# Layer norms of a twelve-block network: the reciprocal root of the variance as a power on GpSimd

## The chip, the cores and the metric

The kernel runs on one core of one Trainium2 chip. The metric is the device time of one launch in microseconds. The profile is one execution of the same program, taken by the hardware profiler.

## What is computed

The input x has shape (32, 32, 128), that is 1024 tokens of 128 features. Twelve blocks in four layers (cross attention, self attention, feed-forward; the feed-forward blocks of layers 0 to 2 mix gated experts) are each added to x, and each takes x normalised over its features:

```python
def _layernorm(x, axis=-1, eps=1e-05):
    m = jnp.mean(x, axis=axis, keepdims=True)
    v = jnp.var(x, axis=axis, keepdims=True)
    return (x - m) / jnp.sqrt(v + eps)
...
x = x + _L3_attn_ref(_layernorm(x, axis=-1), ...)
```

There are six inner norms too. The self attention of layer 3 adds a second norm of its (already normalised) input, with scale and shift, to its output; the self attention of layer 0 normalises its heads' output; the cross attention of layer 2 has two inner norms; the self attention of layer 2 has two that divide by the plain standard deviation (eps 0). With the 12 outer ones that makes 18 norms; "norm 1" to "norm 18" number them in program order. Norm 3 is the inner one of the layer 0 attention, norm 4 that of the layer 0 feed-forward block, norm 15 that of the layer 3 cross attention, and norms 16 and 17 are the two of the layer 3 self attention.

## The kernel before

All activations stay on chip. X, XN, Y, Z and ACC hold the 1024 tokens as 8 tiles of 128 tokens by 128 features (`NT = 8`), tokens on partitions. MV holds mean and variance of each tile (128x8x2), SD two rows of 8 values a partition: the variance plus eps, then the standard deviation and its reciprocal. The order on each engine is written out by hand in five blocks, one an engine, and engines wait for each other only through counted semaphores. So an instruction that waits holds up all that follows it on its engine.

A norm runs like this. VectorE makes the statistics (`bn_stats`, L1327) of 8 tiles and aggregates them (`bn_aggr`, L1336). `layernorm` adds eps to the 8 variances (L1340, raises `var_ready`), waits for `std_ready`, takes the reciprocal (L1343) and writes 8 normalised tiles (L1346). ScalarE's part is `norm_std` (its operations are recorded at L940): it loads the table of the root ahead of time by an operation on one column (`prepare(ACT.Sqrt)`), waits for `var_ready`, takes the root, and prepares the function that the stage wants next. TensorE turns each normalised tile as it comes (`turn`, L431), and ScalarE copies the turned halves to XNT or ZT (L959).

Two norms stand in a particular order. In the layer 0 feed-forward block (norm 4) ScalarE first scales four results of `weight_products(1)`; TensorE's `turn(XN)` waits for the same four (`y_w_taken`). In the layer 3 self attention `self_attention(..., True)` has two norms: ScalarE takes the first root, copies the turned halves, then copies q, k and v out of PSUM (L940, L1174, L1176), and only then takes the second root. VectorE, after the second norm's tiles and two affine operations on Z (L1323), spreads q over the heads in `heads()` (L1323 with a mask as second input, waits for the copy of q), and TensorE's scores (L743) wait for that.

GpSimd (the `@block.gpsimd` block) issues the loads of weights and rows at the start, then runs per stage: the staging of queries (L2022), bias additions to X (`bias`, L2011), expert biases (L2072, L2075), half of the divisions of a softmax (`divide`, L2062) and, in the cross attentions, `spread` (L2093 to L2121). Most of these wait for `norm_ready`, which the 8 tiles of an outer norm raise.

Of the kernel before, what the change touches and what calls it, by code (L numbers as in the profile page):

```python
# [16 lines left out]
ALU = mybir.AluOpType  # L17
ACT = mybir.ActivationFunctionType
# [5 lines left out]
NT = B * S // P  # L24
# [5 lines left out]
DK = 8  # L30
# [4 lines left out]
LN_EPS = 1e-5  # L35
# [84 lines left out]
def perceiver(nc, ctxT, ctxN, fside, mask, wpack, wrows, l1x_w, units, relb, x_in, out):  # L120
    ctx = ExitStack()
    with ctx:
# [6 lines left out]
        X = sb("X", [P, NT, P])  # L129
        XN = sb("XN", [P, NT, P])  # L130
# [32 lines left out]
        def ar(a, n):  # L163
            return AR[:, a:a + n]
# [8 lines left out]
            var_ready std_ready norm_ready stream_ready turned turned_taken  # L173
# [762 lines left out]
        def _(act):  # L936
            seen = Tally(act)

            def f(o, i, fn=ACT.Identity, **k):
                return act.activation(o, i, fn, **k)  # L940

            def prepare(fn):

                f(SM[:, 592:593], ident[:, 0:1], fn).then_inc(sig["act_ran"], 1)
                act.wait_ge(sig["act_ran"], seen.up("act_ran"))

            def norm_std(then=None):

                prepare(ACT.Sqrt)
                act.wait_ge(sig["var_ready"], seen.up("var_ready"))  # L950
                f(SD[:, 1, :], SD[:, 0, :], ACT.Sqrt).then_inc(sig["std_ready"], 1)
                act.wait_ge(sig["std_ready"], seen.up("std_ready"))
                if then:
                    prepare(then)

# [53 lines left out]
            norm_std(ACT.Exp)  # L1009
# [26 lines left out]
            norm_std(ACT.Exp)  # L1036
# [23 lines left out]
            norm_std()  # L1060
# [4 lines left out]
            norm_std(ACT.Sigmoid)  # L1065
# [7 lines left out]
            norm_std(ACT.Exp)  # L1073
# [94 lines left out]
            def self_attention(scale, second_norm=False):  # L1168
                norm_std(None if second_norm else ACT.Exp)
                turned(XNT[:, :])  # L1170
                act.wait_ge(sig["lin_ready"], seen.up("lin_ready"))
                f(c_q, PSF[:, 1024:2048], scale=scale).then_inc(sig["qkv_taken"], 1)
                act.wait_ge(sig["qkv_taken"], seen.up("qkv_taken"))
                act.copy(c_k, PSF[:, 2048:3072]).then_inc(sig["qkv_taken"], 1)  # L1174
                act.wait_ge(sig["qkv_taken"], seen.up("qkv_taken"))
                act.copy(c_vt, PSF[:, 3072:4096]).then_inc(sig["qkv_taken"], 1)  # L1176
                act.wait_ge(sig["qkv_taken"], seen.up("qkv_taken"))
                if second_norm:
                    norm_std(ACT.Exp)
                core()  # L1180
# [5 lines left out]
            norm_std(ACT.Exp)  # L1186
# [65 lines left out]
            norm_std(ACT.Exp)  # L1252
            turned(XNT[:, :])
            cross(None)
            norm_std(LAYERS_FF["l2x"][1])
            turned(ZT[:, :])
            ff("l2x")
            norm_std()


            norm_std(ACT.Exp)
# [22 lines left out]
            norm_std()  # L1284
# [4 lines left out]
            norm_std()  # L1289


            norm_std()
# [12 lines left out]
            norm_std(ACT.Exp)  # L1305
            turned(XNT[:, :])
            cross("l3x_bk")
            self_attention(float(DK) ** -0.5, True)
            norm_std(LAYERS_FF["l3f"][1])
# [9 lines left out]
        def _(dve):  # L1319
# [11 lines left out]
            def layernorm(src, dst, eps, signal=True, stats_done=False):  # L1331

                if not stats_done:
                    stats(src, range(NT))
                for t in range(NT):
                    dve.bn_aggr(MV[:, t, :], ST[:, t, :]).then_inc(sig["dve_ran"], 1)  # L1336
                    seen.up("dve_ran")
                    if t == NT - 1:
                        dve.wait_ge(sig["dve_ran"], seen.up("dve_ran", 0))
                dve.tensor_scalar(SD[:, 0, :], MV[:, :, 1], eps, None, ALU.add).then_inc(sig["var_ready"], 1)  # L1340
                dve.wait_ge(sig["var_ready"], seen.up("var_ready"))
                dve.wait_ge(sig["std_ready"], seen.up("std_ready"))
                dve.reciprocal(SD[:, 1, :], SD[:, 1, :]).then_inc(sig["dve_ran"], 1)  # L1343
# [156 lines left out]
            layernorm(X, XN, LN_EPS)  # L1500
# [42 lines left out]
            layernorm(X, XN, LN_EPS, stats_done=True)  # L1543
# [39 lines left out]
            layernorm(v3(lv), Z, 1e-5, signal=False)  # L1583
# [8 lines left out]
            layernorm(X, XN, LN_EPS, stats_done=True)  # L1592
# [15 lines left out]
            layernorm(X, XN, LN_EPS, stats_done=True)  # L1608
# [142 lines left out]
            layernorm(X, XN, LN_EPS, stats_done=True)  # L1751
# [6 lines left out]
            layernorm(X, XN, LN_EPS, stats_done=True)  # L1758
# [132 lines left out]
            layernorm(X, XN, LN_EPS, stats_done=True)  # L1891
# [6 lines left out]
            layernorm(Y, Z, 1e-5, signal=False, stats_done=True)  # L1898
# [5 lines left out]
            layernorm(ACC, Z, 1e-5, signal=False, stats_done=True)  # L1904
# [7 lines left out]
            layernorm(X, XN, LN_EPS)  # L1912
# [20 lines left out]
            layernorm(Y, Z, 0.0, stats_done=True)  # L1933
# [3 lines left out]
            layernorm(ACC, Y, 0.0, signal=False, stats_done=True)  # L1937
# [4 lines left out]
            layernorm(X, XN, LN_EPS)  # L1942
# [19 lines left out]
            layernorm(X, XN, LN_EPS)  # L1962
# [7 lines left out]
            layernorm(X, XN, LN_EPS, stats_done=True)  # L1970

            layernorm(XN, Z, 1e-5, signal=False)
# [10 lines left out]
            layernorm(X, XN, LN_EPS, stats_done=True)  # L1983
# [8 lines left out]
        def _(pool):  # L1992
            seen = Tally(pool)

            for g in ("l0", "l1", "l2", "l3"):
                a, cols = SPANS["group_" + g]
                if g == "l1":
                    pool.dma_start(RB[:, :, :], wrows.rearrange("a r n -> (a) r n").broadcast_to([P, len(ROWS), P])
                                   ).then_inc(sig["rows_landed"], 16)
                    pool.dma_start(MK[:, 0:2, :], mask[0:2 * P, :].rearrange("(c p) b -> p c b", c=2))\  # L2000
                        .then_inc(sig["mask_landed"], 16)
                    pool.dma_start(MK[:, 2, :], mask[2 * P:KEYS, :].broadcast_to([P, B]))\
                        .then_inc(sig["mask_landed"], 16)
                pool.dma_start(W[:, a:a + cols], wpack[:, a:a + cols]).then_inc(sig["w_" + g], 16)
            pool.wait_ge(sig["w_l0"], 16)
# [24 lines left out]
            seen.up("expert_weights")  # L2030

# [20 lines left out]
            seen.up("yu_taken", 2)  # L2052
            seen.up("norm_ready", NT)
# [26 lines left out]

            pool.wait_ge(sig["norm_ready"], seen.up("norm_ready", NT))
# [63 lines left out]

            pool.wait_ge(sig["norm_ready"], seen.up("norm_ready", NT))
# [6 lines left out]
            spread(False)  # L2153

            divide()
            pool.wait_ge(sig["c_out"], seen.up("c_out", 4))
            for u in range(11, H):
                pool.dma_start(*to_tokens(u)).then_inc(sig["pair_out_pool"], 16)
            seen.up("norm_ready", 2 * NT)


            pool.wait_ge(sig["norm_ready"], seen.up("norm_ready", NT))
# [3 lines left out]

            pool.wait_ge(sig["norm_ready"], seen.up("norm_ready", NT))
            bias("l3x_bo")
            spread(True)
            pool.wait_ge(sig["norm_ready"], seen.up("norm_ready", NT))  # L2170
            bias("l3a_bp")
            divide()
            pool.wait_ge(sig["norm_ready"], seen.up("norm_ready", NT))
# [168 lines left out]
```

## Time and profile before

| | |
|---|---|
| median of 3 runs | 1430.46 us (1424.09 to 1431.08) |
| the profiled execution's own time | 1426.8 us |
| its span in the trace | 1425.0 us |
| busy: TensorE, VectorE, ScalarE, GpSimd | 79%, 53%, 42%, 22% of the span |
| mean granted clock of TensorE | 0.859 of full speed |

The span runs from the first to the last instruction; 1.8 us of the execution's time lie around it. Busy shares are averages over stages with different limits: an engine with 22% can hold up the others wherever they wait for it.

### The profile page before, as it was taken

The numbers are of one execution on the slowest core, as the hardware profiler recorded it, in microseconds if no ns is written. First come the engines' busy times: TensorE is split into PE (matmuls) and PEld (weight loads), VectorE is DVE, ScalarE is ACT, GpSimd is POOL, SyncE is SP. The second block draws the span as 40 slices with busy tenths as digits, with TensorE's granted clock in tenths as the row PEclk, the third lists the DMA queues.
The fourth block names the chain that finished last, engine by engine and source line by source line (L and its number), as shares of the span: only waits on it lengthen the run. The fifth ranks groups of instructions, "written<-read, shape, count | busy, mean of one in ns | idle before, by whom it ended". The sixth has DMA issues, their size and how long they took to land. (4 is left out here: it accounts for less than half of the span.)

```text
span 1425.0 us, 26568 instructions
## 1 busy us (share of the span) xinstructions
PE 1130.6 (79%) x8781; PEld 839.4 (59%) x8781; DVE 750.7 (53%) x2071; ACT 592.0 (42%) x1226; POOL 311.4 (22%) x498
## 2 busy tenths in 40 slices
PE   5758998999996368999965233899999979998537
PEld 2325665878774346788843232577676758886434
DVE  2264444554554944566657494433333346665682
ACT  2133223433432133788842211434444348886122
POOL 1000001111120104555510010404032125554010
PEclk8577998999998568999977566899999989998557
DMA  8510120222220003455500201021111201111000
GB/s 270 142 60 1 35 63 18 57 60 52 56 60 1 2 1 97 120 144 138 148 0 1 45 2 37 28 62 45 45 56 45 71 8 31 30 30 31 1 1 15
DMA packets 70989, 75.04 MB, mean 53 GB/s; under 512 B 6272, under 2 KB 63696, under 8 KB 70536
## 3 DMA queue, kind: packets, MB, share of 16 engines
q1 hardware_dynamic: 67864, 66.18, 17.3%
q0 software_dynamic: 1152, 6.97, 1.4%
q10 hardware_dynamic: 1904, 0.98, 0.4%
q8 instruction: 42, 0.69, 0.2%
q14 instruction: 27, 0.22, 0.0%
HBM read 71.49 MB, written 0.52 MB: 51 GB/s over the span
## 5 line engine op out<-in xcount | busy, mean ns | idle before, releaser
L472 PEld LDWEIGHTS PS<-WB,AR 128*128 128x128 f32 x1568 | 189.4, 192 | 43.6 <-issue 40.7
L472 PE MATMUL PS<-WB,AR 128*128 128x128 f32 x1568 | 189.6, 275 | 0.0
L940 ACT ACTIVATE AR<-PS,WB 128x512 f32<-128x512 f32 x160 | 110.0, 687 | 156.0 <-PE PS L460 149.5
L817 PE MATMUL PS<-AR 128*128 128x257 f32 x512 | 149.3, 395 | 0.1
L1435 DVE SCALAR_TENSOR_TENSOR ACC<-PS,SM,ACC 128x128 f32<-128x128 f32 x256 | 72.2, 345 | 125.7 <-PE PS L472 124.4
L460 PE MATMUL PS<-ZT,WB 128*128 128x512 f32 x208 | 103.8, 624 | 3.5 <-ACT ZT L959 3.5
L817 PEld LDWEIGHTS PS<-AR 128*128 128x128 f32 x512 | 87.7, 191 | 20.0 <-issue 11.1
L1323 DVE TENSOR_TENSOR AR<-PS,AR 128x512 f32<-128x512 f32 (+2 forms) x69 | 48.4, 702 | 91.1 <-issue 39.4
L940 ACT ACTIVATE AR<-PS 128x512 f32<-128x512 f32 (+2 forms) x81 | 43.8, 541 | 121.7 <-PE PS L463 68.0
L460 PE MATMUL PS<-XNT,WB 128*128 128x512 f32 x168 | 89.3, 639 | 5.2 <-ACT AR L940 3.9
L940 ACT ACTIVATE AR<-PS,SM 128x257 f32<-128x257 f32 x136 | 64.8, 476 | 39.3 <-DVE SM L1507 28.8
L431 PE MATMUL PS<-W,XN 128*128 128x128 f32 x96 | 26.6, 450 | 61.9 <-DVE XN L1346 61.9
L940 ACT ACTIVATE AR<-AR 128x1024 f32<-128x1024 f32 (+1 forms) x39 | 46.3, 1188 | 70.0 <-DVE AR L1323 54.2
L754 PE MATMUL PS<-AR 32*32 32x128 f32 x768 | 30.5, 367 | 55.9 <-DVE AR L1725 55.9
L1847 DVE COPY AR<-PS 128x512 f32<-128x512 f32 x64 | 44.3, 692 | 52.6 <-PE PS L826 52.6
L940 ACT ACTIVATE AR<-AR,SM 128x257 f32<-128x257 f32 x128 | 65.3, 510 | 15.9 <-DVE SM L1832 10.5
L2093 POOL TENSOR_TENSOR AR<-AR,W 128x512 f32<-128x512 f32 x64 | 67.0, 1047 | 21.2 <-POOL OT L2121 15.0
L2042 POOL TENSOR_TENSOR AR<-AR,SM 128x516 f32<-128x516 f32 x32 | 33.7, 1054 | 159.1 <-ACT SM L940 93.9
L826 PE MATMUL PS<-W,AR 128*128 128x128 f32 x512 | 66.6, 273 | 2.3 <-ACT AR L940 2.2
L2011 POOL TENSOR_TENSOR X<-X,RB 128x1024 f32<-128x1024 f32 x6 | 14.1, 2345 | 242.8 <-DVE XN L1346 242.5
L2062 POOL TENSOR_TENSOR AR<-AR,SM 128x512 f32<-128x512 f32 x12 | 16.9, 1412 | 221.5 <-DVE SM L1703 221.0
L826 PEld LDWEIGHTS PS<-W,AR 128*128 128x128 f32 x512 | 59.5, 141 | 9.8 <-ACT AR L940 3.5
(225 smaller groups left out, 2207.2 us busy)
## 6 DMA issues: line engine op xcount, KB each, us to landing
WB<-in_units SPq DMA_DIRECT2D x49, 385.0 KB, 3.1
CTX<-in_fside SPq DMA_DIRECT2D x32, 514.0 KB, 4.1
CTX<-in_ctxT SPq DMA_DIRECT2D x96, 130.0 KB, 2.1
CTX<-in_ctxT SPq DMA_DIRECT2D x8, 520.0 KB, 4.5
CTX<-in_ctxN SPq DMA_DIRECT2D x16, 258.0 KB
CTX<-in_ctxN SPq DMA_DIRECT2D x32, 129.0 KB, 2.3
AR<-in_ctxN SPq DMA_DIRECT2D x32, 64.5 KB, 2.9
AR<-in_l1x_w POOLq DMA_DIRECT2D x1, 2048.0 KB, 8.2
```

Source lines behind the costliest of these rows:

```text
L431: m = pe.transpose(PS[:, t // 4, 128 * (t % 4):128 * (t % 4) + 128], src[:, t, :], ident)
L460: m = pe.matmul(bank(2 * c), WB[:, q, 128 * c:128 * c + 128], src[:, 512 * hh:512 * hh + 512], start=True, stop=True)
L472: m = pe.matmul(PS[:, 4 + hh, 128 * t:128 * t + 128], f_h[hh][:, c, 128 * t:128 * t + 128], WB[:, q, 2 * UNIT + 128 * c:2 * UNIT + 128 * c ...
L754: m = pe.matmul(PS[32 * g:32 * g + 32, 4 * half + b, P * tt:P * tt + P], c_vt[32 * b:32 * b + 32, at:at + 32], pt[32 * b:32 * b + 32, g, t ...
L817: m = pe.matmul(PS[:, 2 + g, 0:KEYS], x_qb[q][:, P * g:P * g + P], x_k[q], start=True, stop=True)
L826: m = pe.transpose(PS[:, 6 + c, P * g:P * g + P], x_p[q][:, g, P * c:P * c + P], ident)
L940: return act.activation(o, i, fn, **k)
L1323: return dve.tensor_tensor(o, a, b, op)
L1435: ins = dve.scalar_tensor_tensor(out=a, in0=y, scalar=f_w[:, 4 * hh + t, bass.ds(e, 1)], in1=a, op0=ALU.mult, op1=ALU.add)
L1847: dve.tensor_copy(x_pt[:, 1, :], PS[:, 7, :]).then_inc(sig["xpt_d"], 1)
L2042: pool.tensor_tensor(y_T[k % 2], y_last[k].unsqueeze(1).broadcast_to([P, HG, FQ]), y_pl[:, :, k].unsqueeze(2).broadcast_to([P, HG, FQ]), A ...
L2093: pool.tensor_tensor(x_qb[q].rearrange("p (h q) -> p h q", h=H), qv, m16, ALU.mult)\
```

## The change

Root and reciprocal leave ScalarE and VectorE. GpSimd gets a function `rstd`: when all 8 aggregates are there (each now raises `var_ready`), it adds eps to the variances and raises the sums to the power -0.5, with an exponent tile of eight values -0.5 in SM; VectorE waits for `rstd_ready`. `norm_std` is gone; where it prepared a next function, ScalarE now calls `prepare` alone, without waiting for the variance. In GpSimd's program a call of `rstd` stands for each of the 18 norms, ahead of the wait for that norm's tiles.

```diff
-            def norm_std(then=None):
-
-                prepare(ACT.Sqrt)
-                act.wait_ge(sig["var_ready"], seen.up("var_ready"))
-                f(SD[:, 1, :], SD[:, 0, :], ACT.Sqrt).then_inc(sig["std_ready"], 1)
-                act.wait_ge(sig["std_ready"], seen.up("std_ready"))
-                if then:
-                    prepare(then)
...
-            norm_std(ACT.Exp)
+            prepare(ACT.Exp)
             turned(XNT[:, :])
...
-                if second_norm:
-                    norm_std(ACT.Exp)
                 core()
...
                 for t in range(NT):
-                    dve.bn_aggr(MV[:, t, :], ST[:, t, :]).then_inc(sig["dve_ran"], 1)
-                    seen.up("dve_ran")
-                    if t == NT - 1:
-                        dve.wait_ge(sig["dve_ran"], seen.up("dve_ran", 0))
-                dve.tensor_scalar(SD[:, 0, :], MV[:, :, 1], eps, None, ALU.add).then_inc(sig["var_ready"], 1)
-                dve.wait_ge(sig["var_ready"], seen.up("var_ready"))
-                dve.wait_ge(sig["std_ready"], seen.up("std_ready"))
-                dve.reciprocal(SD[:, 1, :], SD[:, 1, :]).then_inc(sig["dve_ran"], 1)
-                dve.wait_ge(sig["dve_ran"], seen.up("dve_ran"))
+                    dve.bn_aggr(MV[:, t, :], ST[:, t, :]).then_inc(sig["var_ready"], 1)
+                dve.wait_ge(sig["rstd_ready"], seen.up("rstd_ready"))
...
+            def rstd(eps=LN_EPS):
+
+                pool.wait_ge(sig["var_ready"], seen.up("var_ready", NT))
+                pool.tensor_scalar(SD[:, 0, :], MV[:, :, 1], eps, None, ALU.add).then_inc(sig["pool_ran"], 1)
+                pool.wait_ge(sig["pool_ran"], seen.up("pool_ran"))
+                pool.tensor_tensor(SD[:, 1, :], SD[:, 0, :], SM[:, 504:512], ALU.pow).then_inc(sig["rstd_ready"], 1)
+                pool.wait_ge(sig["rstd_ready"], seen.up("rstd_ready"))
+            pool.memset(SM[:, 504:512], -0.5).then_inc(sig["pool_ran"], 1)
+            pool.wait_ge(sig["pool_ran"], seen.up("pool_ran"))
+            rstd()
...
             spread(True)
+            rstd()
             pool.wait_ge(sig["norm_ready"], seen.up("norm_ready", NT))
+            rstd()
             bias("l3a_bp")
```

## Rows read from the trace of the kernel before

**Rows 1.** The page, TensorE's busy time, its share of the span, its instructions.

```profile
PE 1130.6 (79%) x8781; PEld 839.4 (59%) x8781; DVE 750.7 (53%) x2071; ACT 592.0 (42%) x1226; POOL 311.4 (22%) x498
```

**Rows 2.** The tile SD: durations in ns (least/median/most), then its engines' idle time before.

```profile
L1340 DVE TENSOR_SCALAR SD<-MV x18: 171/172/172, 8.1 to 1390.0; 128x8 f32<-128x8 f32 x18
L940 ACT ACTIVATE SD<-SD x18: 208/208/209, 8.4 to 1390.3; 128x8 f32<-128x8 f32 x18
L1343 DVE RECIPROCAL SD<-SD x18: 202/203/204, 8.7 to 1390.6; 128x8 f32<-128x8 f32 x18
...
  DVE SD L1340: 92.7, 16
  ACT SD L940: 19.7, 18
```

**Rows 3.** Timeline of norms 16 and 17: start, duration (us), instruction, idle before.

```profile
1320.51 0.64 DVE L1336 BATCH_NORM_AGGREGATE MV<-ST 128x2 f32<-128x6 f32 x8
...
1322.00 2.14 DVE L1346 TENSOR_SCALAR XN<-X,MV,SD 128x128 f32<-128x128 f32 x8
...
1324.28 2.35 POOL L2011 TENSOR_TENSOR X<-X,RB 128x1024 f32<-128x1024 f32 x1 [10.21 <-DVE XN L1346]
...
1325.85 0.64 DVE L1336 BATCH_NORM_AGGREGATE MV<-ST 128x2 f32<-128x6 f32 x8
...
1333.78 1.02 ACT L940 ACTIVATE AR<-PS 128x1024 f32<-128x1024 f32 x1 [8.44 <-PE PS L765]
...
1335.88 1.01 ACT L1176 COPY AR<-PS 128x1024 f32<-128x1024 f32 x1
...
1337.47 0.20 DVE L1343 RECIPROCAL SD<-SD 128x8 f32<-128x8 f32 x1 [10.77 <-ACT SD L940]
...
1339.88 2.48 DVE L1323 TENSOR_TENSOR Z<-Z,RB 128x1024 f32<-128x1024 f32 x2
1342.40 4.62 DVE L1323 TENSOR_TENSOR AR<-AR,W 128x2048 f32<-128x2048 f32 x2
...
1344.84 0.44 PE L743 MATMUL PS<-AR 32*32 32x128 f32 x4 [11.15 <-DVE AR L1323]
```

**Rows 4.** Timeline of norm 4.

```profile
117.81 0.64 DVE L1336 BATCH_NORM_AGGREGATE MV<-ST 128x2 f32<-128x6 f32 x8
...
119.59 0.60 ACT L940 ACTIVATE AR<-PS 128x512 f32<-128x512 f32 x1 [0.22 <-PE PS L590]
...
120.68 1.28 ACT L940 ACT_TABLE_LOAD   x1
120.76 0.20 DVE L1343 RECIPROCAL SD<-SD 128x8 f32<-128x8 f32 x1 [2.11 <-ACT SD L940]
...
121.50 2.18 PE L431 MATMUL PS<-W,XN 128*128 128x128 f32 x8 [2.00 <-DVE XN L1346]
...
123.77 0.59 ACT L959 COPY XNT<-PS 128x512 f32<-128x512 f32 x1 [0.59 <-PE PS L431]
```

**Rows 5.** Timeline of norm 15, VectorE's reciprocal.

```profile
1150.90 0.20 DVE L1343 RECIPROCAL SD<-SD 128x8 f32<-128x8 f32 x1 [0.79 <-ACT SD L940]
```

**Rows 6.** Timeline of the end of the layer 3 cross attention.

```profile
1312.70 0.25 DVE L1860 SCALAR_TENSOR_TENSOR AR<-PS,SM,AR 128x32 f32<-128x32 f32 x1
1313.09 0.32 POOL L2110 TENSOR_TENSOR AR<-AR 128x64 f32<-128x64 f32 x1 [3.01 <-DVE AR L1860]
1313.49 0.25 POOL L2116 TENSOR_TENSOR AR<-AR 128x32 f32<-128x32 f32 x1
1313.82 0.25 POOL L2121 TENSOR_TENSOR OT<-AR 128x32 f32<-128x32 f32 x1
1314.18 0.75 DVE L1887 TENSOR_SCALAR OT<-OT,W 128x1024 f32<-128x1024 f32 x1 [1.23 <-POOL OT L2121]
```

**Rows 7.** VectorE's groups: count, busy us, mean ns, idle before.

```profile
L1576 DVE RECIPROCAL SM<-SM 128x128 f32<-128x128 f32 x1 | 1.0, 953 | 0.0
```

**Rows 8.** ScalarE's groups: the table loads.

```profile
L940 ACT ACT_TABLE_LOAD x38 | 48.8, 1283 | 12.9 <-issue 5.5 <-PE PS L463 3.4 <-DVE SM L1323 2.7
```

More of the change, by code:

```diff
@@ L172, in perceiver @@
             ctx_rows_landed0 ctx_rows_landed1 unit_landed0 unit_landed1 out_landed
-            var_ready std_ready norm_ready stream_ready turned turned_taken
+            var_ready rstd_ready norm_ready stream_ready turned turned_taken
             lin_ready lin_taken proj_ready bias_ready bias_taken resid_done
@@ L1033, in _ @@
             act.wait_ge(sig["lin_taken"], seen.up("lin_taken"))
-            norm_std(ACT.Exp)
+            prepare(ACT.Exp)
             turned(XNT[:, :])
@@ L1059, in _ @@
             weight_products(0)
-            norm_std()
             turned(ZT[:, :])
             weight_products(1)
-            norm_std(ACT.Sigmoid)
+            prepare(ACT.Sigmoid)
             turned(XNT[:, :])
@@ L1070, in _ @@
             ff("l0f")
-            norm_std(ACT.Exp)
+            prepare(ACT.Exp)
             turned(XNT[:, :])
@@ L1166, in core, with self_attention @@
                             act.wait_ge(sig[name], seen.up(name))
-            def self_attention(scale, second_norm=False):
-                norm_std(None if second_norm else ACT.Exp)
+            def self_attention(scale):
+                prepare(ACT.Exp)
                 turned(XNT[:, :])
@@ L1177, in self_attention @@
                 act.wait_ge(sig["qkv_taken"], seen.up("qkv_taken"))
-                if second_norm:
-                    norm_std(ACT.Exp)
                 core()
             self_attention(float(DK) ** -0.5)
-            norm_std(ACT.Exp)
+            prepare(ACT.Exp)
             turned(XNT[:, :])
@@ L1249, in cross @@
                 seen.up("xu_ready")
-            norm_std(ACT.Exp)
+            prepare(ACT.Exp)
             turned(XNT[:, :])
             cross(None)
-            norm_std(LAYERS_FF["l2x"][1])
+            prepare(LAYERS_FF["l2x"][1])
             turned(ZT[:, :])
             ff("l2x")
-            norm_std()
-            norm_std(ACT.Exp)
+            prepare(ACT.Exp)
             turned(XNT[:, :])
@@ L1283, in _ @@
                 act.dma_start(*to_tokens(u)).then_inc(sig["pair_out_landed"], 16)
-            norm_std()
             turned(ZT[:, :])
@@ L1288, in _ @@
             act.wait_ge(sig["lin_taken"], seen.up("lin_taken"))
-            norm_std()
-            norm_std()
             def gate_exp():
@@ L1302, in _ @@
                 ff("l2f", gate_exp)
-            norm_std(ACT.Exp)
+            prepare(ACT.Exp)
             turned(XNT[:, :])
             cross("l3x_bk")
-            self_attention(float(DK) ** -0.5, True)
-            norm_std(LAYERS_FF["l3f"][1])
+            self_attention(float(DK) ** -0.5)
+            prepare(LAYERS_FF["l3f"][1])
             turned(XNT[:, :])
@@ L1329, in stats, with layernorm @@
                 dve.wait_ge(sig["dve_ran"], seen.up("dve_ran", 0))
-            def layernorm(src, dst, eps, signal=True, stats_done=False):
+            def layernorm(src, dst, signal=True, stats_done=False):
                 if not stats_done:
@@ L1499, in _ @@
             dve.wait_ge(sig["w_first"], 16)
-            layernorm(X, XN, LN_EPS)
+            layernorm(X, XN)
             dve.wait_ge(sig["last_turned"], 1)
@@ L1540, in _ @@
             residual()
-            layernorm(X, XN, LN_EPS, stats_done=True)
+            layernorm(X, XN, stats_done=True)
             dve.wait_ge(sig["w_l0"], 16)
@@ L1582, in _ @@
             dve.wait_ge(sig["dve_ran"], seen.up("dve_ran"))
-            layernorm(v3(lv), Z, 1e-5, signal=False)
+            layernorm(v3(lv), Z, signal=False)
             affine(Z[:, :, :], "l0a_gamma", "l0a_beta").then_inc(sig["dve_ran"], 1)
@@ L1589, in _ @@
             residual()
-            layernorm(X, XN, LN_EPS, stats_done=True)
+            layernorm(X, XN, stats_done=True)
             seen.up("gate_mm")
@@ L1605, in _ @@
             ff("l0f", into=X)
-            layernorm(X, XN, LN_EPS, stats_done=True)
+            layernorm(X, XN, stats_done=True)
             dve.wait_ge(sig["mask_landed"], seen.up("mask_landed", 32))
@@ L1748, in heads @@
                     dve.wait_ge(sig["c_in"], seen.up("c_in"))
-            layernorm(X, XN, LN_EPS, stats_done=True)
+            layernorm(X, XN, stats_done=True)
             dve.wait_ge(sig["w_l1"], 16)
@@ L1755, in _ @@
             residual()
-            layernorm(X, XN, LN_EPS, stats_done=True)
+            layernorm(X, XN, stats_done=True)
             dve.wait_ge(sig["gate_mm"], seen.up("gate_mm", 2))
@@ L1888, in cross @@
                     dve.wait_ge(sig["x_out"], seen.up("x_out"))
-            layernorm(X, XN, LN_EPS, stats_done=True)
+            layernorm(X, XN, stats_done=True)
             dve.wait_ge(sig["w_l2"], 16)
@@ L1897, in _ @@
             residual(Y, XN)
-            layernorm(Y, Z, 1e-5, signal=False, stats_done=True)
+            layernorm(Y, Z, signal=False, stats_done=True)
             affine(Z[:, :, :], "l2x_g1", "l2x_be1").then_inc(sig["stream_ready"], 1)
@@ L1903, in _ @@
             ff("l2x")
-            layernorm(ACC, Z, 1e-5, signal=False, stats_done=True)
+            layernorm(ACC, Z, signal=False, stats_done=True)
             tt(Z[:, :, :], Z[:, :, :], rows_t("l2x_g2"), ALU.mult).then_inc(sig["dve_ran"], 1)
@@ L1909, in _ @@
             dve.wait_ge(sig["resid_done"], seen.up("resid_done"))
-            layernorm(X, XN, LN_EPS)
+            layernorm(X, XN)
             dve.wait_ge(sig["relb_landed"], 64)
@@ L1932, in _ @@
             residual(Y, Y)
-            layernorm(Y, Z, 0.0, stats_done=True)
+            layernorm(Y, Z, stats_done=True)
             tt(ACC[:, :, :], Z[:, :, :], rows_t("l2a_b2"), ALU.add).then_inc(sig["dve_ran"], 1)
@@ L1936, in _ @@
             residual(ACC, ACC)
-            layernorm(ACC, Y, 0.0, signal=False, stats_done=True)
+            layernorm(ACC, Y, signal=False, stats_done=True)
             tt(flat(X), flat(X), flat(Y), ALU.add).then_inc(sig["resid_done"], 1)
             dve.wait_ge(sig["resid_done"], seen.up("resid_done"))
-            layernorm(X, XN, LN_EPS)
+            layernorm(X, XN)
             dve.tensor_copy(flat(ACC), flat(XN)).then_inc(sig["dve_ran"], 1)
@@ L1959, in _ @@
             dve.wait_ge(sig["resid_done"], seen.up("resid_done"))
-            layernorm(X, XN, LN_EPS)
+            layernorm(X, XN)
             dve.wait_ge(sig["w_l3"], 16)
@@ L1967, in _ @@
             residual()
-            layernorm(X, XN, LN_EPS, stats_done=True)
-            layernorm(XN, Z, 1e-5, signal=False)
+            layernorm(X, XN, stats_done=True)
+            layernorm(XN, Z, signal=False)
             affine(Z[:, :, :], "l3a_lng", "l3a_lnb").then_inc(sig["dve_ran"], 1)
@@ L1980, in _ @@
             residual()
-            layernorm(X, XN, LN_EPS, stats_done=True)
+            layernorm(X, XN, stats_done=True)
             dve.memset(flat(ACC), 0.0).then_inc(sig["dve_ran"], 1)
@@ L2025, in _ @@
             bias("l0x_bo")
+            rstd()
             pool.wait_ge(sig["norm_ready"], seen.up("norm_ready", NT))
             pool.dma_start(ar(8192, 4096), l1x_w).then_inc(sig["l1x_w_landed"], 16)
+            rstd()
+            rstd()
             seen.up("norm_ready", NT)
             seen.up("expert_weights")
+            rstd()
             pool.wait_ge(sig["norm_ready"], seen.up("norm_ready", NT))
@@ L2052, in _ @@
             seen.up("yu_taken", 2)
+            rstd()
             seen.up("norm_ready", NT)
@@ L2078, in expert_bias @@
                         pool.wait_ge(sig[name], seen.up(name))
+            rstd()
             pool.wait_ge(sig["norm_ready"], seen.up("norm_ready", NT))
@@ L2143, in spread @@
                     seen.up("x_out")
+            rstd()
             pool.wait_ge(sig["norm_ready"], seen.up("norm_ready", NT))
@@ L2153, in _ @@
             spread(False)
+            rstd()
+            rstd()
+            rstd()
             divide()
@@ L2158, in _ @@
                 pool.dma_start(*to_tokens(u)).then_inc(sig["pair_out_pool"], 16)
+            rstd(0.0)
+            rstd(0.0)
             seen.up("norm_ready", 2 * NT)
+            rstd()
             pool.wait_ge(sig["norm_ready"], seen.up("norm_ready", NT))
@@ L2164, in _ @@
                 expert_bias([f"l2f_b2_{e}" for e in range(4)])
+            rstd()
             pool.wait_ge(sig["norm_ready"], seen.up("norm_ready", NT))
@@ L2169, in _ @@
             spread(True)
+            rstd()
             pool.wait_ge(sig["norm_ready"], seen.up("norm_ready", NT))
+            rstd()
             bias("l3a_bp")
             divide()
+            rstd()
             pool.wait_ge(sig["norm_ready"], seen.up("norm_ready", NT))
```

## The prediction

> **What bounds the kernel now.** I read the page first. TensorE is busy for 79% of the span [rows 1], yet no engine is full: the network is a chain of small stages, and between stages TensorE stands idle until VectorE and ScalarE hand it its next operand. So a layer norm is priced by what lies between the last statistic and the first normalised tile, not by busy time. Next I read the view of the tile SD, which holds every norm's variance and root [rows 2]: 18 times an addition on VectorE (0.17 us), a root on ScalarE (0.21) and a reciprocal on VectorE (0.20). In 16 of the 18 norms ScalarE sat waiting for the variance, so the table of the root had been loaded in time; VectorE waited for the root 19.7 us in all. If all 18 waits were the usual 0.40 us the sum would be 7.2; the timeline shows who holds the other 12.5: norm 17 (10.77 us of wait, [rows 3]), norm 4 (2.11, [rows 4]) and norm 15 (0.79, [rows 5]). I number the norms 1 to 18 in program order.
>
> **An ordinary norm, before.** In norm 16 the last aggregate ends at 1320.51 + 0.64 = 1321.15 and the first XN tile starts at 1322.00 [rows 3]: 0.85 us for addition, hop, root, hop, reciprocal.
>
> **An ordinary norm, after.** The chain becomes: hop VectorE to GpSimd, addition, GpSimd's wait for itself, power, hop to VectorE. The end of a cross attention shows each link on operands of 128x32 and 128x64 [rows 6]. VectorE ends at 1312.70 + 0.25 = 1312.95 and GpSimd starts at 1313.09: 0.14. A dependent GpSimd pair starts 1313.49 after an end at 1313.41: 0.08. GpSimd ends at 1314.07 and VectorE starts at 1314.18: 0.11. A 128x64 operation takes 0.32 and a 128x32 one 0.25, so about 2.2 ns an element over a fixed 0.18; a 128x8 addition is 0.20. With p for the power: 0.14 + 0.20 + 0.08 + p + 0.11 = 0.53 + p. The difference to before is p - 0.32 for each norm on the path.
>
> **The power.** The trace has no power on any engine. From below it is bounded by GpSimd's cheapest two-input operation, 0.25 us [rows 6]; from above I take its 128x1024 addition, 2.35 us [rows 3], as if each of eight powers cost 128 additions. Nearest in kind is VectorE's reciprocal: 0.95 us for 128 elements and 0.20 for 8 [rows 7, 2], 6.2 ns an element, where a product of 1024 elements costs 1.24 us, 1.2 ns an element [rows 3]. So a reciprocal is worth five products. A power is at least a logarithm, a product and an exponential; at five each for the two that is 11 steps of 2.2 ns, 25 ns an element, 0.20 us for eight, and 0.38 with the fixed 0.18. Both functions are probably dearer than a reciprocal, so I take p = 0.5, and keep 0.25 and 2.35 as the ends. VectorE's two small operations take 0.17 and 0.20 [rows 2]; GpSimd's two would be 0.20 and 0.5.
>
> The Trainium skill (GPSIMD Engine Reference, section Engine selection) advises against ordinary elementwise work on GpSimd and puts two-input operations at about twice VectorE's time. By that rule the two operations would be 0.34 and 0.41 us instead of 0.20 and 0.5, and the sum below would come out 0.8 us higher; this trace's GpSimd rows stand at about 1.9 times VectorE's for 1024 elements (2.35 against 1.24).
>
> **Sixteen ordinary norms** (all but 4 and 17), each with TensorE or VectorE's next step waiting for it: 16 x (0.5 - 0.32) = +2.9 us. Ends: 16 x (0.25 - 0.32) = -1.1 and 16 x (2.35 - 0.32) = +32.5. GpSimd is free in each: its next work is queued on the normalised tiles of the same norm, and the parts of the program ahead of each call (staging, divisions, expert biases, the sums of a cross attention) are consumed by VectorE before the statistics can start. I cost no queueing on GpSimd. Norm 15 waits 0.39 longer than the usual for a reason that I don't see in its rows (the root ended in time); I count it as kept, and as gained at the low end.
>
> **Norm 17**, the second norm of the l3 attention. Its variance is ready at 1326.7 us, but ScalarE's root stands in program order behind the three copies of q, k and v, which wait for TensorE and run from 1333.78 to 1336.89; so VectorE's reciprocal starts only at 1337.47 after 10.77 us. Then come eight tiles, two affine operations of 2.48 us together, and at 1342.40 the spreading of q over heads, for which TensorE waits until 1344.84 [rows 3]. With GpSimd taking the root, the aggregate's end at 1326.49 + 1.03 = 1327.5, + 2.2 for the tiles = 1329.7, + 2.5 = 1332.2: all under the cover of the projections. Late next is the copy of q, whose end is 1334.80; the spreading starts at 1334.9 instead of 1342.40: **-7.5 us**. The slack is 2.7 us, so this stays hidden until the power costs 3.2. The bias addition that GpSimd ran at 1324.28 is now queued behind the root and starts near 1327.6; it is wanted only after the attention.
>
> **Norm 4.** ScalarE's root is queued behind four copies of weight products, the last ending at 120.19, so the reciprocal is at 120.76 and TensorE's transposes start at 121.50 [rows 4]. After: statistics end at 118.45, + 1.03 = 119.5, the first tile 0.34 later. Late next are two things released by that last copy: TensorE's own wait (start 120.3, eight transposes of 2.18 us together, end 122.5) and ScalarE's load of the sigmoid's table (1.28 + 0.20 from 120.2, end 121.7). The second copy of the transposed activations starts at 122.6 instead of 123.77: **-1.2 us**. Hidden until p is about 1.1.
>
> **Tables.** ScalarE loads 38 tables [rows 8]. Dropping the root removes its load ahead of most norms and a few that went back to Exp behind it; but ScalarE idled before 16 of 18 roots [rows 2], so these were covered. Cost and gain: nothing. If a load were on the path it would show as 1.28 us each.
>
> **Sum.** +2.9 - 7.5 - 1.2 = -5.8 us. The profiled execution took 1426.8 us and would take 1421.0. The median of the three runs is 1430.46, 3.7 above that execution; I forecast against the median: 1424.7 us. A measurement of this kernel tells about 0.5%, 7.2 us, from no change.
>
> **How it could go instead.**
> *Cheap power (p up to 0.42).* All of the mechanism, and the power near an addition. p = 0.25 gives -1.1 - 7.5 - 1.2 = -9.8: 1420.7 us. For it: the operand is eight elements wide, and fixed costs rule there. Against it: a power must be built of many steps. Chance 0.31.
> *Middling power (0.42 to 1.31).* The forecast, -5.8. Own range 1423.3 to 1437.6. Chance 0.35.
> *Dear power: slower.* One mechanism, at every ordinary norm: VectorE and TensorE wait on GpSimd for p. The change is even when 16 x (p - 0.32) = 8.7, at p = 0.86, and slower by over 0.5% from p = 1.31 (8.7 + 7.2 = 15.9 = 16 x 0.99). At 2.35 it gives +32.5 - 8.7 = +23.8: 1454.3 us. For it: (1.31 - 0.18) / 8, some 140 ns an element, suffices, and no power in the trace excludes that. Chance 0.27.
> *Norm 17 gives nothing.* If the stage is held by something else, say by the spreading waiting on another copy, the sum is +1.7: 1432.2 us. For it: k and v are copied until 1336.89. Against it: the spreading waits for q alone. Chance 0.07. The same number would follow if the change did not take the root out of ScalarE's queue.
>
> **Range and chances.** From 1417 (the cheap end, norm 15's 0.4 and 3 us for runs that scatter over 7) to 1445 (a power of 1.75 us); what is left out is some 0.17 above and 0.02 below. Faster by over 0.5% is the cheap case with a little of the middling one, 0.33; within 0.5% the rest of the middling one and the case without norm 17, 0.40; slower 0.27.
>
> **What the changed kernel's profile would show.** Rows of GpSimd on SD, 18 additions near 0.20 us and 18 powers: their duration decides everything. The time from the last aggregate to the first XN tile, 1.03 if I am right. In the l3 attention, Z tiles straight after the second aggregates, and VectorE idle before the spreading until the copy of q. Fewer table loads, near 20. The prediction is wrong if the power lies outside 0.4 to 0.9, if hops to GpSimd from an idle wait are longer than 0.14, or if the shorter gaps in TensorE's work change the clock that it is granted behind them.

## The result and the profile after

The changed kernel takes 1443.24 us in the median of 4 runs (1441.25 to 1448.72), the kernel before, run beside it, 1430.14. The ratio is 1.0107, with a 95% interval of 1.0068 to 1.0146: **13 us slower**. The forecast of 1424.7 was wrong. The time lies inside the range, near its upper end, in the rival called "dear power", which had a chance of 0.27.

The view of the tile SD in the changed kernel, against [rows 2]:

```profile
L1986 POOL TENSOR_SCALAR SD<-MV x18: 234/238/240, 8.5 to 1404.7; 128x8 f32<-128x8 f32 x18
L1988 POOL TENSOR_TENSOR SD<-SD,SM x18: 1665/1665/1681, 8.9 to 1405.0; 128x8 f32<-128x8 f32 x18
...
L1323 DVE TENSOR_SCALAR Z<-XN,MV,SD x8: 333/335/2470, 1350.8 to 1354.8; 128x128 f32<-128x128 f32 x8
...
  POOL SD L1988: 39.2, 18
```

The power takes 1.665 us, each of 18 times. VectorE now waits 39.2 us for it in all; for the root on ScalarE it waited 19.7, of which 10.77 fell to norm 17 alone. The row of Z shows one tile of 2.47 us among tiles of 0.34; I come back to it.

The timeline of norms 16 and 17, against [rows 3]:

```profile
1341.32 0.64 DVE L1320 BATCH_NORM_AGGREGATE MV<-ST 128x2 f32<-128x6 f32 x8
1342.12 0.24 POOL L1986 TENSOR_SCALAR SD<-MV 128x8 f32<-128x8 f32 x1 [7.24 <-DVE MV L1320]
1342.44 1.67 POOL L1988 TENSOR_TENSOR SD<-SD,SM 128x8 f32<-128x8 f32 x1
1344.14 2.14 DVE L1323 TENSOR_SCALAR XN<-X,MV,SD 128x128 f32<-128x128 f32 x8 [2.18 <-POOL SD L1988]
...
1348.00 0.64 DVE L1320 BATCH_NORM_AGGREGATE MV<-ST 128x2 f32<-128x6 f32 x8
...
1350.85 4.26 DVE L1323 TENSOR_SCALAR Z<-XN,MV,SD 128x128 f32<-128x128 f32 x8 [2.21 <-POOL SD L1988]
1350.89 2.34 POOL L1999 TENSOR_TENSOR X<-X,RB 128x1024 f32<-128x1024 f32 x1
...
1355.15 2.48 DVE L1307 TENSOR_TENSOR Z<-Z,RB 128x1024 f32<-128x1024 f32 x2
1355.35 1.02 ACT L940 ACTIVATE AR<-PS 128x1024 f32<-128x1024 f32 x1 [7.87 <-PE PS L765]
...
1357.66 4.62 DVE L1307 TENSOR_TENSOR AR<-AR,W 128x2048 f32<-128x2048 f32 x2
```

Norm 16 is an ordinary norm: the last aggregate ends at 1341.96 and the first tile starts at 1344.14, 2.18 us, where it was 0.85. Norm 17's 10.77 us of wait is gone. From norm 16's first aggregate to the spreading of q (L1307 with W) it took 21.89 us before and takes 16.34 now, 15.01 without norm 16's own 1.33: norm 17 gives back 6.9 us.

The timeline of norm 4, against [rows 4]:

```profile
117.54 6.51 PE L590 MATMUL PS<-AR 64*128 64x128 f32 x32
...
119.35 0.64 DVE L1320 BATCH_NORM_AGGREGATE MV<-ST 128x2 f32<-128x6 f32 x8
...
122.17 2.14 DVE L1323 TENSOR_SCALAR XN<-X,MV,SD 128x128 f32<-128x128 f32 x8 [2.18 <-POOL SD L1988]
...
124.14 0.60 ACT L940 ACTIVATE AR<-PS 128x512 f32<-128x512 f32 x1 [1.11 <-PE PS L590]
124.75 1.28 ACT L940 ACT_TABLE_LOAD   x1
124.79 1.97 PE L431 MATMUL PS<-W,XN 128*128 128x128 f32 x8 [0.75 <-ACT AR L940]
```

Here the order came out as argued: TensorE's transposes start right behind the fourth copy of the weight products, and the sigmoid's table is loaded behind it. But that copy ends late, because TensorE needed 6.51 us for the 32 products of L590. The stretches of these products in the view by windows, the kernel before first (columns: length, then busy time and instructions of each engine; TensorE's granted clock, as a share of 2.4 GHz, is the third number from the right):

```profile
116.00:119.50 3.50, 3.49 (x33) 3.30 (x32) 2.45 (x15) 1.79 (x3) 0.00 (x0) 1.00 0.00 0
```

and the changed kernel:

```profile
117.54:124.05 6.51, 6.50 (x33) 6.21 (x32) 4.15 (x22) 1.79 (x3) 1.90 (x2) 0.50 0.00 1
```

The clock is 1.2 GHz in place of 2.4. It did not fall at this point: in both kernels it stood at 1.2 GHz for the transposes and products ahead (0.51 from 112.29 to 116.00 us before, 0.50 from 113.82 to 117.54 now), and only in the kernel before did it rise at their end. ScalarE's table loads, against [rows 8], fell to about the number that was forecast (near 20), and the time did not fall with them:

```profile
L940 ACT ACT_TABLE_LOAD x20 | 25.7, 1283 | 7.1 <-PE PS L463 3.4 <-DVE SM L1307 2.7 <-PEq L2323 0.7
```

### The profile page after: what moved, and what is told of

Read it like the earlier page. It is cut to its first block and busy times, and to the rows that moved or that the text cites. A ratio compares the mean times of both kernels' runs of the same rounds, so it can differ in the third digit from the quotient of the medians.

```text
span 1439.0 us, 26495 instructions
## 1 busy us (share of the span) xinstructions
PE 1128.6 (78%) x8781; PEld 839.2 (58%) x8781; DVE 746.0 (52%) x2035; ACT 561.1 (39%) x1172; POOL 346.3 (24%) x535
## 5 line engine op out<-in xcount | busy, mean ns | idle before, releaser
L472 PEld LDWEIGHTS PS<-WB,AR 128*128 128x128 f32 x1568 | 189.4, 192 | 43.5 <-issue 39.2
L1307 DVE TENSOR_TENSOR AR<-PS,AR 128x512 f32<-128x512 f32 (+2 forms) x69 | 48.4, 701 | 91.6 <-issue 39.3
L1986 POOL TENSOR_SCALAR SD<-MV 128x8 f32<-128x8 f32 x18 | 4.3, 238 | 362.8 <-DVE MV L1320 362.8
L940 ACT ACTIVATE AR<-AR,SM 128x257 f32<-128x257 f32 x128 | 65.3, 510 | 15.9 <-DVE SM L1809 10.6
L431 PEld LDWEIGHTS PS<-W,XN 128*128 128x128 f32 x96 | 17.6, 186 | 86.4 <-issue 46.6
```

Source lines behind the costliest of these rows:

```text
L431: m = pe.transpose(PS[:, t // 4, 128 * (t % 4):128 * (t % 4) + 128], src[:, t, :], ident)
L472: m = pe.matmul(PS[:, 4 + hh, 128 * t:128 * t + 128], f_h[hh][:, c, 128 * t:128 * t + 128], WB[:, q, 2 * UNIT + 128 * c:2 * UNIT + 128 * c ...
L1307: return dve.tensor_tensor(o, a, b, op)
```

## Experiments

### The power replaced by a product

```diff
-                pool.tensor_tensor(SD[:, 1, :], SD[:, 0, :], SM[:, 504:512], ALU.pow).then_inc(sig["rstd_ready"], 1)
+                pool.tensor_tensor(SD[:, 1, :], SD[:, 0, :], SM[:, 504:512], ALU.mult).then_inc(sig["rstd_ready"], 1)
...
-            pool.memset(SM[:, 504:512], -0.5).then_inc(sig["pool_ran"], 1)
+            pool.memset(SM[:, 504:512], 0.02).then_inc(sig["pool_ran"], 1)
```

> The changed kernel with the power replaced by a product with 0.02 (so the norms are scaled wrongly: the root is left out); every wait stays. Theory A (the power's own 1.67 us is the loss, passed on in full by 16 norms): the product takes 0.20, each gap from the last aggregate to the first tile falls from about 2.2 to about 0.8 us, and the time is 1443.2 - 16 x 1.47 = about 1420, 0.7% below the kernel before. Theory B (the loss is the hops to GpSimd and what is queued there, the power only a part): gaps stay above 1.2 us and the time stays above 1430.

The root is left out, so what this kernel puts out is not the network's result; only its time is used. Measured: 1416.93 us, ratio to the kernel before 0.9918 (0.9897 to 0.9939). Norm 16 in its timeline:

```profile
1317.89 0.64 DVE L1320 BATCH_NORM_AGGREGATE MV<-ST 128x2 f32<-128x6 f32 x8
1318.70 0.23 POOL L1986 TENSOR_SCALAR SD<-MV 128x8 f32<-128x8 f32 x1 [7.20 <-DVE MV L1320]
1319.01 0.20 POOL L1988 TENSOR_TENSOR SD<-SD,SM 128x8 f32<-128x8 f32 x1
1319.25 2.14 DVE L1323 TENSOR_SCALAR XN<-X,MV,SD 128x128 f32<-128x128 f32 x8 [0.71 <-POOL SD L1988]
```

Two hops to another engine, an addition and a product cost 0.72 us from 1318.53 to 1319.25, less than the 0.85 of the kernel before. Gaps lie at 0.64 to 0.75 in all 18 norms. Theory A holds, theory B falls: hops and GpSimd's queue are not the loss, the power's own time is. With p = 0.20 the prediction's own formula gives 16 x (0.20 - 0.32) - 8.7 = -10.6 us; measured is -0.82%, -11.7.

### The power twice

```diff
+                pool.tensor_tensor(SM[:, 512:520], SD[:, 0, :], SM[:, 504:512], ALU.pow).then_inc(sig["pool_ran"], 1)
+                pool.wait_ge(sig["pool_ran"], seen.up("pool_ran"))
                 pool.tensor_tensor(SD[:, 1, :], SD[:, 0, :], SM[:, 504:512], ALU.pow).then_inc(sig["rstd_ready"], 1)
```

> The changed kernel with a second, discarded power ahead of the real one in each norm. Theory A: 1.67 + 0.08 us more in each of 16 norms, and norm 17, whose cover is used up by now, pays too: 17 x 1.75 = 30 us over the changed kernel, about 1473, ratio to the kernel before 1.030. Rival (a part of the norms has cover: transfers in the first cross attention, the weight products in norm 4): 20 us or less, below 1464.

Measured: 1477.1 us (1473 expected), ratio 1.035 (1.0324 to 1.0376), 34 us above the changed kernel by the medians; the profiled spans, 1469.5 against 1439.0, differ by 30.5. The two powers in the view of the tile SD:

```profile
L1988 POOL TENSOR_TENSOR SM<-SD,SM x18: 1665/1665/1681, 8.7 to 1431.9; 128x8 f32<-128x8 f32 x18
L1990 POOL TENSOR_TENSOR SD<-SD,SM x18: 1635/1635/1640, 10.5 to 1433.6; 128x8 f32<-128x8 f32 x18
```

Each gap grew by 1.71 us, to 3.83 to 3.95. The rival's 20 us are exceeded: nearly all of what a norm costs more is paid at the end.

### Powers of other widths

```diff
+            pool.memset(SM[:, 1084:1140], 0.7).then_inc(sig["pool_ran"], 1)
+            pool.wait_ge(sig["pool_ran"], seen.up("pool_ran"))
+            for n, op in ((1, ALU.pow), (4, ALU.pow), (8, ALU.pow), (16, ALU.pow), (32, ALU.pow), (8, ALU.mult),
+                          (8, ALU.add)):
+                pool.tensor_tensor(SM[:, 1140:1140 + n], SM[:, 1084:1084 + n], SM[:, 1084:1084 + n], op)\
+                    .then_inc(sig["pool_ran"], 1)
+                pool.wait_ge(sig["pool_ran"], seen.up("pool_ran"))
```

> The changed kernel with five extra powers of 128x1, 128x4, 128x8, 128x16 and 128x32 and a product and a sum of 128x8, one after the other on GpSimd where it idles before norm 15; nothing waits for them. If the power costs by the element (a loop over the row): with 1.67 us at 8 and a fixed 0.2, 0.18 us an element: 0.4, 0.9, 1.7, 3.1 and 6.1 us. Rival (a fixed start of about 1.4 us, little by the element): 1.4 at one element and under 2.5 at 32. Product and sum: 0.20 each.

One execution, 1448.93 us; nothing waits for the extra operations, and only their durations are used. GpSimd's groups (count, busy us, mean ns):

```profile
L2169 POOL TENSOR_TENSOR SM<-SM 128x32 f32<-128x32 f32 x1 | 5.4, 5416 | 0.1
...
L2169 POOL TENSOR_TENSOR SM<-SM 128x16 f32<-128x16 f32 x1 | 2.9, 2895 | 0.1
L2169 POOL TENSOR_TENSOR SM<-SM 128x8 f32<-128x8 f32 x3 | 2.0, 680 | 0.2
L2169 POOL TENSOR_TENSOR SM<-SM 128x4 f32<-128x4 f32 x1 | 1.0, 1010 | 0.1
L2169 POOL TENSOR_TENSOR SM<-SM 128x1 f32<-128x1 f32 x1 | 0.6, 563 | 0.1
```

The group of three holds the power, the product and the sum of 128x8; the shortest took 0.202 us, and two of that leave 1.64 for the power, as in the norms. From 4 to 32 elements it costs (5.416 - 1.010) / 28 = 0.157 us an element over a fixed 0.4. The cost goes by the element, so the rival of a long fixed start falls. It is some 75 times what an addition costs an element: 2.1 ns, from 0.251 us for 128x32 and 2.345 for 128x1024 in the trace of the kernel before. The base and exponent were 0.7 here and the variance and -0.5 in the norms, with the same time at 8 elements; no other values were tried.

### Only the order of ScalarE's queue: norm 17, and norms 4 and 17

Both are edits of the kernel before; GpSimd has no part.

```diff
                 turned(XNT[:, :])
+                if second_norm:
+                    norm_std(ACT.Exp)
...
                 act.wait_ge(sig["qkv_taken"], seen.up("qkv_taken"))
-                if second_norm:
-                    norm_std(ACT.Exp)
                 core()
```

> The kernel before, with ScalarE's second root of the layer 3 self attention ahead of the copies of q, k and v; nothing on GpSimd. If norm 17's stall is only the order of ScalarE's queue: the spreading over heads starts when q is copied, 7.5 us earlier, 1422.6, ratio 0.9948. Rival (the time is given back by the scores, the softmax or a lower TensorE clock): within 3 us of the kernel before, ratio above 0.998.

Measured: 1420.13 us, ratio 0.9944 (0.9927 to 0.9961), 8 us faster. Its timeline:

```profile
1325.31 2.14 DVE L1346 TENSOR_SCALAR Z<-XN,MV,SD 128x128 f32<-128x128 f32 x8
...
1330.42 1.02 ACT L940 ACTIVATE AR<-PS 128x1024 f32<-128x1024 f32 x1 [3.94 <-PE PS L765]
1331.47 1.01 ACT L1176 COPY AR<-PS 128x1024 f32<-128x1024 f32 x1
1331.54 4.62 DVE L1323 TENSOR_TENSOR AR<-AR,W 128x2048 f32<-128x2048 f32 x2 [1.58 <-ACT AR L940]
```

The spreading now starts with the copy of q, as the prediction said of what is late next. From norm 16's first aggregate to it this profile has 13.08 us in place of 21.89. That is 8.8 less, of which 1.3 is TensorE's: its eight products of L439 took 5.18 us here and 6.50 in the kernel before. The gain that the changed kernel owes to GpSimd in norm 17 needs no GpSimd: moving one call does it, without the power.

The second edit adds norm 4:

```diff
-            def weight_products(m_out):
+            def weight_products(m_out, root_before=None):
...
                 for k in range(4):
+                    if k == root_before:
+                        norm_std()
                     act.wait_ge(sig["y_w_ready"], seen.up("y_w_ready"))
...
-            weight_products(1)
-            norm_std(ACT.Sigmoid)
+            weight_products(1, 3)
+            prepare(ACT.Sigmoid)
```

> The same, and in norm 4 ScalarE's root ahead of the fourth copy of the weight products. If norm 4's queue is worth its 1.2 us as predicted: 1421.4, ratio 0.9940, and TensorE's transposes of norm 4 start about 1.2 us sooner after the last aggregate. Rival (norm 4's transposes wait for the copies, not for the root, or the slower clock of the weight products takes it): no change against the run with norm 17 alone.

Measured: 1421.43 us, ratio 0.9953 (0.9927 to 0.998). The timeline of norm 4:

```profile
119.24 0.21 ACT L940 ACTIVATE SD<-SD 128x8 f32<-128x8 f32 x1
119.48 0.60 ACT L940 ACTIVATE AR<-PS 128x512 f32<-128x512 f32 x1
...
120.28 2.03 PE L431 MATMUL PS<-W,XN 128*128 128x128 f32 x8 [1.18 <-DVE XN L1348]
```

From the first aggregate to the transposes it is 3.02 us, where the kernel before takes 3.69 [rows 4]: 0.7 us in place. The expectation was 1.2. From norm 4's last aggregate to norm 5's it is 109.24 us, in the kernel before 110.06 and with norm 17 alone 110.26, so the gain reached norm 5 in this profile. The times can't tell this kernel from the one with norm 17 alone; whether the gain reaches the end stays open. In norm 17's stretch, with L439 at 6.67 us, it has 14.57 in place of 21.89: 7.3 less.

### Norm 17 alone on GpSimd

```diff
+                if on_pool:
+                    for t in range(NT):
+                        dve.bn_aggr(MV[:, t, :], ST[:, t, :]).then_inc(sig["var17_ready"], 1)
+                    dve.wait_ge(sig["rstd_ready"], seen.up("rstd_ready"))
...
+            pool.wait_ge(sig["var17_ready"], NT)
+            pool.tensor_scalar(SD[:, 0, :], MV[:, :, 1], LN_EPS, None, ALU.add).then_inc(sig["pool_ran"], 1)
...
+            pool.tensor_tensor(SD[:, 1, :], SD[:, 0, :], SM[:, 504:512], ALU.pow).then_inc(sig["rstd_ready"], 1)
```

ScalarE's second root is gone with it, and the table of the exponential is prepared right behind the first.

> The kernel before with norm 17 alone on GpSimd (addition and power as in the changed kernel), the other 17 norms as before. If the changed kernel is one gain of about 7 us and seventeen small losses: 6.9 to 7.5 us below the kernel before, ratio about 0.995, like the early root on ScalarE. Rival (the power on GpSimd costs more than its wait, in the clock or by the shared work): above 0.998.

Measured: 1423.36 us, ratio 0.9959 (0.9944 to 0.9974): 5.9 us faster, and the rival's 0.998 is excluded. So the changed kernel is one gain here and the losses of the other norms. It is less than expected by 1 us or so, and its timeline has the long tile too:

```profile
1333.19 4.26 DVE L1349 TENSOR_SCALAR Z<-XN,MV,SD 128x128 f32<-128x128 f32 x8 [2.22 <-POOL SD L2179]
1333.24 2.34 POOL L2014 TENSOR_TENSOR X<-X,RB 128x1024 f32<-128x1024 f32 x1
```

### GpSimd's bias ahead of norm 17's root

```diff
+            bias("l3a_bp")
             rstd()
-            bias("l3a_bp")
             divide()
```

> The changed kernel with GpSimd's bias addition ahead of the root of norm 17 instead of behind it. If the 2.47 us tile of VectorE there is a wait for that addition: no Z tile of norm 17 above 0.35 us, the eight take 2.14 instead of 4.26, and the spreading over heads starts about 1.2 us sooner, held then by the copy of q. Rival (the long tile has another cause): it stays.

One execution, 1440.91 us. Its timeline:

```profile
1347.29 2.35 POOL L1999 TENSOR_TENSOR X<-X,RB 128x1024 f32<-128x1024 f32 x1 [2.32 <-DVE XN L1323]
...
1351.75 2.14 DVE L1323 TENSOR_SCALAR Z<-XN,MV,SD 128x128 f32<-128x128 f32 x8 [2.25 <-POOL SD L1988]
...
1355.87 1.02 ACT L940 ACTIVATE AR<-PS 128x1024 f32<-128x1024 f32 x1 [7.53 <-PE PS L765]
...
1357.00 4.62 DVE L1307 TENSOR_TENSOR AR<-AR,W 128x2048 f32<-128x2048 f32 x2 [0.60 <-ACT AR L940]
```

The eight tiles are back at 2.14 us and the spreading starts 14.83 us after norm 16's first aggregate (1342.17), 1.5 sooner than in the changed kernel (16.34), held by the copy of q. Of the 1.5 us, 0.3 is that copy itself, which ended 14.72 us after the aggregate here and 15.05 in the changed kernel; the other 1.2 is the tile, as expected. So the long tile, the first of the eight, was held by the bias addition, which by the recorded starts began 0.04 us behind it. In all seven profiles in which the addition starts beside norm 17's first tile, the one with the product among them, that tile takes 2.47 us. The same addition beside VectorE's statistics (L1311, 1.64 us for eight, 1.65 without it) slows nothing.

The Trainium skill (SBUF — State Buffer, section Who interferes with whom) says that VectorE's `tensor_scalar` can enter a mode with two ports and then shares a locked port pair with GpSimd for a whole instruction. This trace agrees: one tile took 2.470 us beside a GpSimd instruction of 2.34. The runs show the wait and its length, not the port.

### Does norm 3 decide TensorE's clock in norm 4?

Three kernels, one execution each: norm 3 alone on GpSimd, with the same edit as for norm 17; the changed kernel with norm 3 alone back on ScalarE and VectorE; and the changed kernel once more.

> The kernel before with norm 3 alone on GpSimd. Its gap from the last aggregate to the first tile is 2.1 instead of 0.85 us. If the longer wait there is what left the weight products of norm 4 at TensorE's lower clock (6.51 instead of 3.50 us): they run at 1.2 GHz here too and norm 5's aggregates come 4 us later than in the kernel before. Rival (the clock there differs from execution to execution, as in the run of power widths): about 3.5 us, and norm 5 comes 1.3 us later.

> The changed kernel with norm 3 alone back on ScalarE and VectorE. If norm 3's wait decides the clock: weight products in 3.5 us at 2.4 GHz. Rival (chance of the execution): either.

> The changed kernel once more, unchanged. If its clock in the weight products of norm 4 is a property of the program: 6.51 us again. Rival (chance of the execution): 3.5 to 6.5 us, and the norms' gaps the same as in the first profile to 0.05 us.

They took 1435.03, 1441.37 and 1443.01 us, the kernel before beside them 1424.08; single executions can't settle the few us at stake here, so only the rows are used. Their weight products of norm 4, norm 3 alone on GpSimd:

```profile
116.34 4.08 PE L590 MATMUL PS<-AR 64*128 64x128 f32 x32
...
121.14 1.28 ACT L940 ACT_TABLE_LOAD   x1
...
122.67 0.21 ACT L940 ACTIVATE SD<-SD 128x8 f32<-128x8 f32 x1
```

norm 3 back on ScalarE:

```profile
117.58 3.50 PE L590 MATMUL PS<-AR 64*128 64x128 f32 x32
```

the changed kernel again:

```profile
122.37 6.51 PE L590 MATMUL PS<-AR 64*128 64x128 f32 x32
```

and the run of power widths, which is the changed kernel up to there:

```profile
121.42 3.50 PE L590 MATMUL PS<-AR 64*128 64x128 f32 x32
```

The changed program up to that point was profiled four times (the first profile, the two just named, and the run with the bias moved): 6.51, 6.51, 3.50 and 6.51 us. With a gap of 0.85 or less at norm 3 it was 3.50 to 3.69 in all seven kernels. With norm 3 alone on GpSimd it was 4.08, at a granted clock of 0.84, and with the power twice, where norm 3's wait is longest, 3.60. So the low clock was seen only with a longer wait at norm 3, and not each time; the expectation that this wait alone decides falls, and what decides stays open. The price where it occurs: from norm 4's first tile to norm 5's last aggregate 109.5 us in place of 107.5.

The kernel with norm 3 alone on GpSimd shows one thing more. ScalarE's part of norm 3 had loaded the table that norm 4's root needs; without it the load stands behind the fourth copy, and TensorE's transposes start 2.59 us after that copy's end (123.71), in the kernel before 1.31. So a table load that nothing covers cost its 1.28 us in full here, as the prediction said of a load on the path.

### Eps inside the root

The early roots of norms 4 and 17, and in each norm the addition taken out; the aggregates raise `var_ready` themselves:

```diff
-                f(SD[:, 1, :], SD[:, 0, :], ACT.Sqrt).then_inc(sig["std_ready"], 1)
+                f(SD[:, 1, :], MV[:, :, 1], ACT.Sqrt, bias=eps).then_inc(sig["std_ready"], 1)
...
-                dve.tensor_scalar(SD[:, 0, :], MV[:, :, 1], eps, None, ALU.add).then_inc(sig["var_ready"], 1)
-                dve.wait_ge(sig["var_ready"], seen.up("var_ready"))
```

> The kernel with ScalarE's early roots in norms 4 and 17, and eps given to the root as its bias instead of an addition on VectorE in each norm. The addition and its step are 0.21 us; the bias as an operand may take back 0.1. Gaps from the last aggregate to the first tile fall from 0.85 to 0.65 to 0.75; 18 x 0.1 to 0.2 = 2 to 4 us below the run with the early roots, ratio to the kernel before 0.992 to 0.994.

Measured: 1417.53 us, ratio 0.9928 (0.9909 to 0.9947): by its median the fastest kernel here that computes the reference, though its interval overlaps those of the two with early roots alone. Norm 16:

```profile
1318.56 0.64 DVE L1338 BATCH_NORM_AGGREGATE MV<-ST 128x2 f32<-128x6 f32 x8
1319.30 0.30 ACT L940 ACTIVATE SD<-MV,SM 128x8 f32<-128x8 f32 x1 [9.86 <-DVE MV L1338]
1319.63 0.20 DVE L1340 RECIPROCAL SD<-SD 128x8 f32<-128x8 f32 x1 [0.43 <-ACT SD L940]
1319.87 2.14 DVE L1343 TENSOR_SCALAR XN<-X,MV,SD 128x128 f32<-128x128 f32 x8
```

The root with a bias in a tile takes 0.30 in place of 0.21 us, the addition is gone, and the gap is 0.67 in place of 0.85. Over the 18 norms the gaps are 3.9 us shorter in its profile than in the one with both early roots, 0.6 of that in norm 15; the medians of the two differ by 3.9 as well, but the times of the one with both early roots spread over 10 us (1416.18 to 1426.67), so that agreement proves little.

## Why the prediction was wrong

- **The step that failed** is the size of p: 0.5 us was taken, 1.67 measured, between the ends 0.25 and 2.35. I built it from VectorE's reciprocal: two functions at five products each, 11 steps of 2.2 ns, 25 ns an element. The run of widths showed 157 ns, six times that, and close to the 140 ns which the rival of the dear power said would suffice. A sum built from a reciprocal on VectorE said nothing of a power on GpSimd. With 1.67 in its own formula the prediction gives 16 x (1.67 - 0.32) - 8.7 = +12.9 us; measured is 13.1. That the two numbers agree to 0.2 us is in part luck: the profile of the changed kernel has -6.9 for norm 17 instead of -7.5, and from norm 4's last aggregate to norm 5's +1.7 (111.72 against 110.06) instead of -1.2. With 16 x 1.33 that makes +16.1, and the two profiled spans differ by 14.0.
- **The links of the chain** were right. 0.53 + 1.67 = 2.20 was forecast for the gap from last aggregate to first tile, 2.12 to 2.23 measured. With the product 0.73 was due and 0.72 came. Single links are off by little: the addition takes 0.24 for 0.20, and GpSimd's end to VectorE's start is 0.03, not 0.11.
- **Sixteen norms on the path**: supported by the run with two powers, 1.71 us more a gap and 30.5 more in the span, and by the product; neither tells the norms apart. The Trainium skill (GPSIMD Engine Reference, section Engine selection) gives its factor of two for two-input operations and calls one-input ones roughly line-rate. The prediction put the factor on the addition of eps as well, which has one input: that took 0.24 us against VectorE's 0.17, 1.4 times. For the power the factor gave 0.41 and 1.67 was measured, eight times VectorE's reciprocal.
- **Norm 17**: mechanism right, -7.5 forecast, -6.9 in the profile of the changed kernel. Missing is the cost of moving the bias addition: I saw that it would start near 1327.6 and asked only who waits for its result, not whom it blocks while it runs. Here that took 2.1 us of a slack that the power had already cut to 1.5, which leaves 0.6 on the path: 7.5 - 0.6 = 6.9.
- **Norm 4**: the order is as forecast, but the -1.2 us did not come in this execution, because the weight products ran at half the clock. The prediction named a changed clock as a sign of being wrong, for shorter gaps, and gave it no price. In an execution without that (the run of widths) norm 5's last aggregate came 109.69 us after norm 4's, in the kernel before 110.06: a gain of 0.4. The prediction's own limit (hidden until p is 1.1) leaves 0.6 at a power of 1.67.
- **Norm 15's** extra 0.39 us was counted as kept, and is absent after the change. Of the five kernels that leave norm 15 as it was, four show it (VectorE waits 0.79 us in each), and the one with only norm 3 on GpSimd does not (0.40). Its cause stays open.
- **Tables**: 18 fewer loads brought no gain that any row shows, as argued.
- **The rest**: stages that the change leaves alone differ by as much as 5 us between executions of one program. From norm 1's first tile to norm 2's last aggregate it is 64.3 us in the kernel before, and 60.6, 61.9, 64.7 and 65.4 in four executions of the changed one. So whether norm 1's own 1.4 us reach the end can't be read here.

## What to carry to other kernels

An operation that no row shows should be measured alone before eighteen copies of it are put on the path: a single kernel with five widths would have given the one number that decided this case. Where a short step waits long, look first at what stands ahead of it in its engine's queue: one moved call gave 8 us, more than the 5.9 that the same norm gave on GpSimd. (Even with a product for the power, all 18 norms on GpSimd gave 11.7.) And a step that moves to another engine moves what is queued behind it there; ask whom that work blocks, not only who needs it.

## What the runs showed of the hardware

- A power of fp32 on GpSimd takes 0.56 us for 128x1, 1.01 for 128x4, 1.67 for 128x8, 2.90 for 128x16 and 5.42 for 128x32: 0.4 us and 0.157 more for each element of a row. A sum or product of 128x8 takes 0.20.
- Two hops over GpSimd with two cheap operations (0.72 us) are no dearer than the hops over ScalarE with three (0.85).
- One VectorE tile of 128x128, started by the trace 0.04 us ahead of a two-input GpSimd instruction of 128x1024, took 2.47 us in place of 0.34, and the GpSimd instruction kept its 2.34; statistics beside the same instruction kept their time (1.64 us for eight).
- A load of ScalarE's table takes 1.28 us, and the path grew by 1.28 where nothing covered it.
- A root of 128x8 takes 0.21 us without a bias and 0.30 with the bias in a tile.
- The same program up to one point ran 32 products at 2.4 GHz in one execution and at 1.2 GHz in three, 3.50 and 6.51 us.
